# Forming two rows' score maxima inside the mixer: eight in its last full step, eight in its tail

## What is computed

```python
x = _layernorm(x + mixer(x))                  # gated linear recurrence, 32 heads, 128 states
x = _layernorm(x + cross_attention(x, ctx))   # 32 query heads, 8 key/value heads of width 8
x = _layernorm(x + experts(x))                # 8 experts, top 2, and a shared one
```

```python
scores = jnp.einsum('bkgsd,bktd->bkgst', qh, kh) * scale
attn = jax.nn.softmax(scores, axis=-1)
out = jnp.einsum('bkgst,bktd->bkgsd', attn, vh)
```

## Time and profile before

| what | value |
|---|---|
| time, median of 3 runs | 747.63 us (747.26 to 751.16) |
| time of the profiled execution | 746.63 us |
| its span, first to last instruction | 744.6 us |
| mean granted TensorE clock | 0.997 |
| TensorE matmul busy | 719.3 us (97%) |
| VectorE busy | 572.9 us (77%) |
| ScalarE busy | 442.7 us (59%) |
| GpSimd busy | 379.6 us (51%) |

### The profile page before, as it was taken

One profiled execution on the slowest core, in us unless ns is written; L12 is line 12 of the kernel. 1 busy time (PEld: TensorE's weight loads), 2 busy tenths in 40 slices (PEclk: granted clock), 3 DMA queues, 4 the chain that ended last, 5 costly groups with the idle time before them and its releaser, 6 DMA issues. The chain is left out here.

```text
span 744.6 us, 17072 instructions
## 1 busy us (share of the span) xinstructions
PE 719.3 (97%) x5866; PEld 396.9 (53%) x5874; DVE 572.9 (77%) x1104; ACT 442.7 (59%) x870; POOL 379.6 (51%) x420
## 2 busy tenths in 40 slices
PE   8899999999999999999999999999979999999897
PEld 3455555555555555565555556565633334335464
DVE  5677868687686868668686868879689999897887
ACT  7844546654454675445467554455646777778676
POOL 2877527473352747334274964556320341377654
PEclk9999999999999999999999999999999999999999
DMA  6585332224532222552221343422003300000001
GB/s 206 185 223 182 76 57 56 65 48 100 177 75 56 57 62 51 99 175 78 56 56 58 85 107 58 102 61 59 1 15 129 104 23 24 24 0 3 29 30 56
DMA packets 34297, 57.90 MB, mean 78 GB/s; under 512 B 7056, under 2 KB 11920, under 8 KB 33680
## 3 DMA queue, kind: packets, MB, share of 16 engines
q1 hardware_dynamic: 33680, 57.08, 29.4%
q10 hardware_dynamic: 576, 0.31, 0.1%
HBM read 54.10 MB, written 2.36 MB: 76 GB/s over the span
## 5 line engine op out<-in xcount | busy, mean ns | idle before, releaser
L292 POOL TENSOR_TENSOR cum_rows<-cum_rows,cum_t 128x512 f32<-128x512 f32 x128 | 136.9, 1080 | 192.8 <-DMA cum_rows<-cum_scratch 192.8
L808 PE MATMUL pring<-xt_hi,w_hi 128*128 (+1 forms) x576 | 171.8, 380 | 0.0
L808 PE MATMUL pring<-xt_hi,w_lo 128*128 (+1 forms) x576 | 171.3, 379 | 0.0
L808 PE MATMUL pring<-xt_lo,w_hi 128*128 (+1 forms) x576 | 171.3, 379 | 0.0
L660 DVE TENSOR_TENSOR bt<-pring,bt 128x512 f16<-128x512 f32 x128 | 88.1, 688 | 72.3 <-ACT bt L449 72.3
L449 ACT CAST bt<-pring 128x512 f16<-128x512 f32 x128 | 74.6, 583 | 111.8 <-PE pring L808 111.5
L664 DVE TENSOR_TENSOR ct<-pring,ct 128x512 f16<-128x512 f32 x128 | 88.2, 689 | 54.0 <-ACT ct L453 53.8
L850 PEld LDWEIGHTS pscore<-ct,bt 128*128 128x128 f16 x1536 | 96.0, 98 | 34.5 <-issue 6.7
L850 PE MATMUL pscore<-ct,bt 128*128 128x128 f16 x1536 | 106.6, 219 | 3.7 <-DVE mt L632 2.3
L453 ACT CAST ct<-pring 128x512 f16<-128x512 f32 x128 | 74.8, 585 | 52.5 <-PE pring L808 52.5
L808 PEld LDWEIGHTS pring<-xt_lo,w_hi 128*128 128x128 f16 x576 | 56.3, 98 | 68.1 <-issue 0.3
(11 more groups left out here) (169 smaller groups left out, 950.9 us busy)
## 6 DMA issues: line engine op xcount, KB each, us to landing
cum_rows<-cum_scratch SPq DMA_DIRECT2D x32, 1024.0 KB, 7.9
w_raw<-in_w_in SPq DMA_DIRECT2D x35, 256.0 KB, 6.5
q_rows<-in_xt SPq DMA_DIRECT2D x4, 512.0 KB, 10.7
acc<-in_x SPq DMA_DIRECT2D x1, 2048.0 KB, 7.6
vals<-in_vals SPq DMA_DIRECT2D x16, 128.0 KB, 2.1
out<-acc SPq DMA_DIRECT2D x7, 256.0 KB, 2.2
w_raw_e<-in_w_up SPq DMA_DIRECT2D x1, 1024.0 KB, 5.8
w_raw_e<-in_w_gate SPq DMA_DIRECT2D x1, 1024.0 KB, 4.8
```

Source lines behind the costliest of these rows:

```text
L292: nc.gpsimd.tensor_tensor(rows[:, par, :, q], rows[:, par, :, q], own, ALU.subtract).then_inc(sem("since"), 1)
L808: mm = nc.tensor.matmul(bank[name][:], w[:, c, k, cols], x[:, k, bass.ds(n % TB, 1), :].rearrange("p o n -> p (o n)"), start=(i == 0), sto ...
```

## The change

Row 0's eight score banks are formed in the last full step of the mixer, in the two `pscore` banks, before the projections listed in `max_places` (slot and B or C). VectorE's last full step is written out, outside its loop, and reduces each bank before the low part of the same name. TensorE waits for the reductions (`maxima_read`) where it overwrites such a bank. At the tail's start row 0's maxima are transposed into `pring[1]`, and ScalarE negates them before `evac_q(8)`; the output projection waits for that. The tail's eight banks, reductions, transpose and negation are now row 1's. SyncE's instruction that stores row 0's maxima is unchanged, and waits for the first negation. In the attention block the eight D, eight reductions, X and negation of row 1 are gone from the opening, which has the eight F of row 0 and the eight D of row 2; SyncE's list there begins with the store of row 1's maxima.

```diff
+        late_max = [pring[2], pring[3], pscore[1]]
+        mx_t = [pring[1][0:32, 0:L], pring[2][0:32, 0:L]]
+        max_places = [(3, "B"), (3, "C"), (4, "B"), (4, "C"), (5, "B"), (6, "B"), (6, "C"), (7, "B")]
+        def max_bank(i):
+            s, k = max_places[i]
+            return pscore[(s + (k == "C")) % 2]
...
@@ ScalarE, mixer @@
+            negate_max(0)
             evac_q(8)
             evac_q(9)
             high_y(STEPS)
             evac_q(10)
             evac_q(11)
-            act.wait_ge(sem("mx_turn"), 1)
-            nc.scalar.mul(neg_mx[:, 0], mx_t, -1.0).then_inc(sem("neg_max"), 1)
+            negate_max(1)
...
@@ VectorE, mixer @@
+            def first_row_max(i):
+                dve.wait_ge(sem("max_mm"), i + 1)
+                nc.vector.tensor_reduce(mx[:, 0, :, i], max_bank(i)[:].rearrange("p (k n) -> p k n", k=4), AX.X, ALU.max).then_inc(sem("max_red"), 1)
...
+                for s in range(3, SLOTS):
+                    if maxima:
+                        for i in maxima_at(s, "B"):
+                            first_row_max(i)
                     low_b(n, s)
+                    if maxima:
+                        for i in maxima_at(s, "C"):
+                            first_row_max(i)
                     low_c(n, s)
                     weigh(n, s - 1)
...
-            with dve.Fori(STEPS - TB + 1, STEPS) as n:
+            with dve.Fori(STEPS - TB + 1, STEPS - 1) as n:
                 step(n, norm=True)
+            step(STEPS - 1, norm=True, maxima=True)
...
@@ TensorE, mixer @@
+            def maxima_read(pe, bank_, below):
+                last = max([i for i in range(below) if max_bank(i) is bank_], default=-1)
+                if last >= 0:
+                    pe.wait_ge(sem("max_red"), last + 1)
+            def first_row_scores(n, i):
+                s, k = max_places[i]
+                pe.wait_ge(sem("mixed"), 8 * n + s + (3 if k == "B" else 4))
+                if i == 0:
+                    pe.wait_ge(sem("k_load"), 16 * 28)
+                maxima_read(pe, max_bank(i), i)
+                nc.tensor.matmul(max_bank(i)[:], q_rows[:, 0, i // 4, i % 4, :], k_rows[:, 0, i // 4].rearrange("p k n -> p (k n)"),
+                                 start=True, stop=True).then_inc(sem("max_mm"), 1)
...
                 for s in range(1, SLOTS):
-                    pair(n, s)
+                    for k, half in (("B", 0), ("C", 1)):
+                        for i in maxima_at(s, k) if maxima else ():
+                            first_row_scores(n, i)
+                        project(n, f"{k}{s}", s + 1, half, ("b_proj", "c_proj")[half])
+                    if maxima:
+                        maxima_read(pe, pscore[s % 2], len([p for p in max_places if p[0] <= s]))
                     scores(n, s - 1)
...
             scores(STEPS, -1)
-            pe.wait_ge(sem("k_load"), 16 * 28)
+            pe.wait_ge(sem("c_evac"), 8 * STEPS + 1)
+            turn_max(0)
             for i in range(3):
                 for_max(i)
...
+            pe.wait_ge(sem("neg_max"), 1)
             out_project(STEPS, last=True)
             for_max(7)
             turn_q(11)
-            pe.wait_ge(sem("max_red"), 8)
-            nc.tensor.transpose(mx_t, mx[:, 0].rearrange("p k i -> p (k i)"), ident[:]).then_inc(sem("mx_turn"), 1)
+            turn_max(1)
...
@@ SyncE, attention block @@
+            store_max(1, 1)
             load_values(0, 0)
             load_values(1, 1)
-            store_max(1, 1)
...
@@ ScalarE, VectorE, attention block @@
-            negate_max(1, 1)
...
-            for i in range(8):
-                row_max(1, 1, i, early=True)
...
@@ TensorE, attention block @@
-            for i in range(4):
-                for_max(1, i, early=True)
-            for i in range(3):
-                shifted(0, 0, i)
-            for i in range(4, 8):
-                for_max(1, i, early=True)
-                if i < 7:
-                    shifted(0, 0, i - 1)
+            for what in "D0 D1 F0 F1 F2 D2 F3 D3 F4 D4 F5 D5 F6 D6 F7 D7".split():
+                (shifted(0, 0, int(what[1])) if what[0] == "F" else for_max(2, int(what[1])))
             times_values(0, 0, 0)
-            shifted(0, 0, 6)
-            shifted(0, 0, 7)
-            for_max(2, 0)
-            for_max(2, 1)
-            turn_max(1, 1)
-            for i in range(2, 8):
-                for_max(2, i)
```

More of the change, by code:

```diff
@@ L142, in mixer, with maxima_at @@
         mx, neg_mx = heads["mx"], heads["neg_mx"]
-        first_max = [pring[2], pring[3], pscore[1]]
-        mx_t = pring[2][0:32, 0:L]
+        late_max = [pring[2], pring[3], pscore[1]]
[4 more added lines that the diff above has]
+            return pscore[(s + (k == "C")) % 2]
+        def maxima_at(s, k):
+            return [i for i, place in enumerate(max_places) if place == (s, k)]
         def consumed(eng, name, n):
@@ L553, in _, with negate_max @@
             step(STEPS - TB + 3, queries=range(4, 8))
+            def negate_max(b):
+                act.wait_ge(sem("mx_turn"), b + 1)
+                nc.scalar.mul(neg_mx[:, b], mx_t[b], -1.0).then_inc(sem("neg_max"), 1)
+            negate_max(0)
             evac_q(8)
@@ L737, in first_step, with step @@
                 dve.wait_ge(sem("cw_half"), 3)
-            def step(n, norm=False):
+            def first_row_max(i):
+                dve.wait_ge(sem("max_mm"), i + 1)
+                nc.vector.tensor_reduce(mx[:, 0, :, i], max_bank(i)[:].rearrange("p (k n) -> p k n", k=4), AX.X, ALU.max).then_inc(sem("max_red"), 1)
+            def step(n, norm=False, maxima=False):
                 convolve(n, 0)
@@ L758, in step @@
                 add_out(n, 1)
[L759 to L763, removed]
+                for s in range(3, SLOTS):
+                    if maxima:
+                        for i in maxima_at(s, "B"):
+                            first_row_max(i)
                     low_b(n, s)
+                    if maxima:
+                        for i in maxima_at(s, "C"):
+                            first_row_max(i)
                     low_c(n, s)
                     weigh(n, s - 1)
+                    if s == 3:
+                        pad_values(n)
+                        continue
                     if norm:
@@ L773, in _ @@
                 step(n)
-            with dve.Fori(STEPS - TB + 1, STEPS) as n:
+            with dve.Fori(STEPS - TB + 1, STEPS - 1) as n:
                 step(n, norm=True)
+            step(STEPS - 1, norm=True, maxima=True)
             def row_max(i):
-                dve.wait_ge(sem("max_mm"), i + 1)
-                nc.vector.tensor_reduce(mx[:, 0, :, i], first_max[i % 3][:].rearrange("p (k n) -> p k n", k=4), AX.X, ALU.max).then_inc(sem("max_red"), 1)
+                dve.wait_ge(sem("max_mm"), 8 + i + 1)
+                nc.vector.tensor_reduce(mx[:, 1, :, i], late_max[i % 3][:].rearrange("p (k n) -> p k n", k=4), AX.X, ALU.max).then_inc(sem("max_red"), 1)
             weigh(STEPS, -1)
@@ L926, in turn_q, with step @@
                 mm.then_inc(sem("q_turn_mm"), 1)
-            def step(n, queries=()):
+            def maxima_read(pe, bank_, below):
[10 more added lines that the diff above has]
+                                 start=True, stop=True).then_inc(sem("max_mm"), 1)
+            def step(n, queries=(), maxima=False):
                 project(n, "val", 0, 0, "val_proj")
@@ L954, in _, with turn_max @@
             step(STEPS - 2, range(0, 4))
-            step(STEPS - 1, range(4, 8))
+            step(STEPS - 1, range(4, 8), maxima=True)
+            def turn_max(b):
+                pe.wait_ge(sem("max_red"), 8 * b + 8)
+                nc.tensor.transpose(mx_t[b], mx[:, b].rearrange("p k i -> p (k i)"), ident[:]).then_inc(sem("mx_turn"), 1)
             def for_max(i):
@@ L963, in for_max @@
                 else:
[L964 to L967, removed]
+                    pe.wait_ge(sem("max_red"), 8 + i - 2)
+                q = q_rows[:, 1:2, i // 4, i % 4, :].rearrange("p o n -> p (o n)")
+                k = k_rows[:, 1:2, i // 4].rearrange("p o k n -> p (o k n)")
+                nc.tensor.matmul(late_max[i % 3][:], q, k, start=True, stop=True).then_inc(sem("max_mm"), 1)
             scores(STEPS, -1)
-            pe.wait_ge(sem("k_load"), 16 * 28)
+            pe.wait_ge(sem("c_evac"), 8 * STEPS + 1)
+            turn_max(0)
             for i in range(3):
@@ L1373, in evac_query, with row_max @@
                 nc.vector.tensor_copy(q_rows[:, late + i].rearrange("p t g n -> p (t g) n"), turned).then_inc(sem("q_rows"), 1)
-            def row_max(b, slot, i, early=False):
+            def row_max(b, slot, i):
                 dve.wait_ge(sem("max_mm"), 8 * b + i + 1)
-                scores = early_max[i % 4] if early else max_bank(i)
-                nc.vector.tensor_reduce(mx[:, slot, :, i], scores[:].rearrange("p (k n) -> p k n", k=4), AX.X, ALU.max).then_inc(sem("max_red"), 1)
```

(7 more changed lines are left out.)

1 line of the change is left out of this document (removed).

## The result

The changed kernel takes 742.54 us (median of 12 runs, 741.44 to 747.05) against 746.73 us for the kernel before (median of 12, among them the three runs behind the 747.63 us of the table above). The ratio is 0.9947, 95% interval 0.993 to 0.9964. The profiled execution took 742.52 us with a span of 740.7 us; that of before 746.63 us and 744.6 us.

A forecast was written before the change was run, and what follows sets the result against it. TensorE, busy 97% of the span, was taken to bound the kernel. With the clock kept, + 2.40 (last step) - 0.9 (block end) - 5.76 (opening) = -4.3 us, forecast 743.4 us against the median; range 742.0 to 746.2 us.

The forecast's parts named there:

- X: Transpose of row 2's maxima in the attention block, at T + 11.66 before; whatever moves it moves the rest of the kernel.
- Row 0's matmuls: Mixer's last full step: eight score matmuls at 0.216 us each cost TensorE 1.73 us, with nothing to hide them.
- The stop in slot 5: Mixer's last full step: TensorE waits 0.67 us before scores(4) for VectorE's fifth reduction, which comes late.
- The tail: After the last full step: VectorE sets its length; the added transpose and negation cost nothing, 0.2 us without cover.
- T: The first matmul of the attention block, at 552.02 us in the profile of the kernel before.
- The end of the block: Between mixer and attention block: row 0's store leaves early, SyncE's drain is no longer last, 0.9 us less standing.
- The opening: Attention block's start: eight matmuls and reductions fewer bring X 5.76 us earlier with clock kept, 4.46 us with it lost.
- The clock: Rival at the attention block's opening: TensorE's clock falls again after the stand, giving 744.7 us; chance 0.37 including never lost before.
- the two cases: Attention block's opening: clock kept, -4.3 us, chance 0.42; clock lost as before, -3.0 us, chance 0.37 including never lost before.
- The prediction's other guess: Opening of the kernel before: timed runs not slowed as the profiled one, X at about T + 10.2, gain near 3 us.
- VectorE was late: Rival in the last full step: reductions late in every slot before scores(2) to scores(6), 748.9 us if all exposed; chance 0.06.
- Row 1's store and the values: Attention block's opening: store there at T + 2.4, wanted at T + 4.4 or later; values 0.7 us later; neither costs anything.

The follow-up runs named there:

- the doubled kernel: The changed kernel with each of row 0's eight score matmuls issued twice in the last full step; 744.11 us, ratio 0.997 to before.
- the late store: The changed kernel, but SyncE's store of row 0's maxima waits for the second negation, so is the block's last instruction again; 744.81 us, ratio 0.9989 to before.
- the fifth experiment: The changed kernel run again without edit, beside more executions of the kernel before; 742.37 us, ratio 0.9957 to before.
- the stand filled: The kernel before with six unused 512-column matmuls at the end of TensorE's list in the mixer; 745.12 us, ratio 0.9985 to before.
- row 0 alone: The changed mixer without row 1's maxima work in the tail, attention block as before the change; 747.03 us, ratio 1.0017 to before.
- F0 first: The changed kernel with slot 5's place moved, four unused matmuls at the mixer's end, and opening order F0 D0 D1; 741.41 us, ratio 0.9934 to before.

## Why the prediction was right, point by point

The forecast, 743.4 us, was 0.9 us above the measured median. That distance is the base's: the median of three runs of before, 747.63, lay 0.9 us above that of twelve, 746.73. The forecast change was -4.3 us in the profiled execution and -4.2 by the medians; measured were -4.1 and -4.2. Some of that closeness is luck. The join came out 0.1 us better than forecast and the opening 0.17 us worse. And the sum sets an execution of before that lost the clock against one of after that kept it, which holds for the medians only in part.

*Row 0's matmuls* were to cost 1.73 us and do: the doubled kernel measures 0.216 us each. *The stop in slot 5* was worked out as 0.67 us and is 0.66 (531.12 to 531.78), from the chain that was named; moving one place takes it away. Together the last step is 2.40 us longer, as written down.

*The tail* was costed at nothing, and the step from scores(7) to T is shorter by 1.00 us, the block end's part. What the prediction did not see is how little the eight reductions weigh there. It called the tail's length VectorE's, but without row 1's maxima the tail is just 1.09 us shorter, held by the queries of row 11.

*The end of the block* was to give 0.9 us. It gave 1.00, and the late store brings 0.99 back.

*The opening* was to put X at T + 5.9 with the clock kept and at T + 7.2 with it lost. It was T + 6.07 in the profiled execution, and T + 7.37 in the kernel with the late store. Both are 0.17 us late, and with the clock kept it is the bound that was wrong. The prediction gave TensorE's sixteen matmuls 3.5 us, called them "not the bound", and took X from the end of ScalarE's eighth exponential, T + 5.4. ScalarE was faster than that, its exponentials (4.03 - 0.60) / 7 = 0.49 us apart and not 0.57; the eighth ended at T + 4.87 and nothing before X waited for it. The longest of the waits that did count is D2's, seen at its weight load (PEld):

```profile
554.67 4.03 ACT L1329 ACTIVATE probs<-bank_at 128x512 f32<-128x512 f32 x8 [0.73 <-PE bank_at L1653]
...
555.06 0.10 PEld L1644 LDWEIGHTS bank_at<-k_rows,q_rows 128*128 128x128 f16 x1 [0.49 <-DVE mx L1427]
...
557.51 0.38 PE L1644 MATMUL bank_at<-k_rows,q_rows 128*128 128x512 f16 x1
...
557.82 1.07 PE L1661 MATMUL bank_at<-probs,vals 128*32 128x512 f32 x8
```

X came from TensorE's own list. D2 and D3 waited for a reduction and start 0.38 and 0.34 us after the matmul in front of them, not 0.22; F3, F6 and F7 waited for an exponential, about 0.04 us each; and the product with the values starts 0.31 us after D7 (557.51 to 557.82; before the change, 556.50 to 556.81). So from T to the product it is 3.99 us, not 3.5; then come the product, 1.0 us, and five matmuls, 1.1 us. At the prediction's own prices that list would have ended at T + 5.6, so the nearness of 5.9 is in part luck: TensorE's list was put 0.5 us too short and ScalarE's too long. With the clock lost TensorE's list was the bound, as forecast; D7 came at T + 4.97 (forecast 4.9) and the product 0.31 us behind it instead of 0.2.

*The clock* was the open point between the two cases, and the first of them came true in the profiled execution. For the runs as a whole it was no clean alternative: before, most executions lost the clock at the join; after, half have a mean clock of 0.998 or less, but none of the four profiled with a stand of 1.33 us lost it there. The prediction's other guess, that X of the kernel before would stand near T + 10.2 with the clock kept, was T + 10.30 when tried. At equal clock the change is worth 3.3 us by the runs of the fifth experiment, 2.8 us by the trace (2.40 - 1.00 - 4.23, with X of before at T + 10.30), near the 3 us that the prediction gave for this case. The rest of the measured 4.2 us is put down to the clock, which fits its price of 1.36 us but was not measured apart.

*The rivals.* VectorE was late in one slot, not in all. Row 1's store and the values were not waited for in the opening: from T to X TensorE stands for neither.

What stays open: five of 24 executions of the changed kernel take 746 to 747 us with a mean clock of 0.995, which is more loss than one low spell like that of the opening before (mean 0.997). None of them was profiled. The one long execution that was, of the kernel before with the stand filled, had lost its 3.0 us in the mixer's first 58 us, so the join is not the only suspect.

## What to carry to other kernels

Work that a saturated engine must do anyway is best moved beside the idle time of the *other* engine that it needs: here row 0's matmuls cost full price in a step that TensorE fills, and what paid was taking sixteen serial reductions down to eight where TensorE waited for them. Half of such a move can be worth nothing: with row 0 alone the kernel was no faster (ratio 1.0017, 1.0003 to 1.003), since the tail that it freed was held by something else.

Look at who drains last at a join of all engines. A small store at the end of an idle queue cost 1.0 us of standing, and in the profiled execution the clock that was lost behind it another 1.3 us.

A mean clock over a whole execution does not say where the clock was lost. Before it is put down to one stretch, the stretch's own window has to show it.

## What the runs showed of the hardware

Stands of TensorE of about 2.3 us can cost the clock, and their length alone doesn't decide it. At the join of the blocks the clock fell to its lower level, 1.2 GHz, within about 1 us of the first matmul in both profiled executions with a stand of 2.3 us, and in none of the eight with 0.46 to 1.51 us. At the mixer's start a stand of 2.33 us cost it in one execution, while stands of 2.30 to 2.34 us at the same place left it at 2.4 GHz in three others (the kernel before, F0 first, and the doubled matmuls). Six matmuls whose result nobody reads, put into the stand at the join, raised the executions with a mean clock of 0.999 or more from 2 of 29 to 7 of 11.

A low spell costs what the stretch lets it cost: 1.30 us and 1.36 us in the two openings, next to nothing at the mixer's start in the fifth experiment.

Issuing a small strided store takes SyncE 0.71 us, and its drain 0.46 us more, before a block can end. ScalarE's drain ends with its last instruction: with row 0 alone, copy and drain both end at 551.4.
